# Moving a norm and an expert's sum to VectorE, and a setup loop into the first turn, of a hybrid S6 / mixture-of-experts / S5 kernel

## What is computed

```python
x = x + S6(layernorm(x))      # selective scan, then a norm with gamma and beta of its own
x = x + MOE(layernorm(x))     # 8 experts of hidden size 256, the two largest logits weigh them
x = x + S5(layernorm(x))      # diagonal complex scan with 64 states
x = x + MOE(layernorm(x))     # the same expert weights again
```

## Time and profile before

| | |
|---|---|
| median of 3 executions | 1848.97 us (1846.12 to 1856.43) |
| profiled execution | 1861.63 us, span of its instructions 1859.7 us |
| first scan to end of last | 55.05 to 1696.1 us |
| DVE / POOL busy | 1514.5 / 1513.9 us (81% each) |
| PE / ACT busy | 1351.0 / 1281.5 us |

### The profile page before, as it was taken

The page is one execution under the profiler, slowest core; times in us unless marked ns, Lnnn a source line. Parts: engine busy times, 40 slices in busy tenths (PEclk is TensorE's granted clock), DMA queues, the critical chain, the costliest instruction groups (busy, mean ns, idle before and its releaser), DMA issues.

```text
span 1859.7 us, 19053 instructions
## 1 busy us (share of the span) xinstructions
PE 1351.0 (73%) x5928; PEld 617.7 (33%) x5928; DVE 1514.5 (81%) x2105; ACT 1281.5 (69%) x2275; POOL 1513.9 (81%) x888
## 2 busy tenths in 40 slices
PE   4336458777886887778776878778787778668958
PEld 1001123234342343324342343324332343324535
DVE  4879988898889889898899888888888988895222
ACT  4547668687877778777777778777787777755423
POOL 0899999978998799977998899987998799983312
PEclk9557569889987989879897989879898898979979
DMA  3601411122111311132101401132111321100000
GB/s 87 212 34 71 164 46 51 49 91 97 57 40 48 148 51 33 54 104 96 55 25 50 162 29 51 49 106 81 51 51 49 102 85 52 46 29 1 7 1 6
DMA packets 38747, 121.89 MB, mean 66 GB/s; under 512 B 5875, under 2 KB 21110, under 8 KB 26358
## 3 DMA queue, kind: packets, MB, share of 16 engines
q1 hardware_dynamic: 37062, 120.67, 18.3%
q10 hardware_dynamic: 1584, 0.01, 0.0%
HBM read 109.13 MB, written 11.53 MB: 65 GB/s over the span
## 4 chain that ended last, share of the span: by engine, by line
PE 27%; ACT 18%; DVE 15%; POOL 14%; issue 8%; DVEq 0%; POOLq 0%; ACTq 0%
DVE h L1251 10%; POOL w L947 9%; PE bankH L565 8%; ACT da L837 5%; PE bankY L579 5%; PE bankG L565 5%; ACT yk L798 4%; ACT L837 3%; PE ys L633 2%; POOL x L890 2%; PE bankG L512 2%; DVE aq L1189 1%; PE bankY L559 1%; ACT L785 1%; ACT sq L785 1%
## 5 line engine op out<-in xcount | busy, mean ns | idle before, releaser
L1251 DVE TENSOR_TENSOR_SCAN h<-da,w 128x512 f32<-128x512 f32 x1024 | 1192.1, 1206 | 158.3 <-ACT da L837 133.0
L947 POOL TENSOR_TENSOR w<-ur,br 128x1024 f32<-128x1024 f32 x512 | 1193.6, 2365 | 33.1 <-DVE h L1251 21.2
L837 ACT ACTIVATE da<-dr,al 128x511 f32<-128x511 f32 x1024 | 681.9, 687 | 221.9 <-DVE h L1251 212.5
L633 PE MATMUL ys<-h,wsum 128*32 128x512 f32 x2048 | 320.9, 703 | 208.5 <-DVE h L1251 189.2
L565 PE MATMUL bankH<-nT,w 128*128 128x512 f32 x512 | 301.8, 673 | 89.7 <-DVE aq L1189 85.3
L890 POOL TENSOR_TENSOR x<-x,yk 128x512 f32<-128x512 f32 x128 | 163.1, 1274 | 211.2 <-ACT yk L798 210.6
L579 PEld LDWEIGHTS bankY<-w,aq 128*128 128x128 f32 x2048 | 262.8, 203 | 87.0 <-issue 65.0
L579 PE MATMUL bankY<-w,aq 128*128 128x128 f32 x2048 | 270.5, 289 | 12.4 <-DVE aq L1189 7.9
L565 PE MATMUL bankG<-nT,w 128*128 128x512 f32 x432 | 243.8, 648 | 24.6 <-DVE aq L1189 24.6
L798 ACT ACTIVATE yk<-bankY,rt 128x128 f32<-128x128 f32 x512 | 151.8, 364 | 121.5 <-PE bankY L579 107.8
L633 PEld LDWEIGHTS ys<-h,wsum 128*32 128x32 f32 x2048 | 42.9, 115 | 408.5 <-DVE h L1251 373.2
(11 more groups left out here) (187 smaller groups left out, 1135.8 us busy)
## 6 DMA issues: line engine op xcount, KB each, us to landing
br<-b_rows SPq DMA_DIRECT2D x64, 1024.0 KB, 5.0
dr<-d_rows SPq DMA_DIRECT2D x16, 1024.0 KB, 7.1
ur<-u_rows SPq DMA_DIRECT2D x16, 1024.0 KB, 8.4
d_rows<-vh SPq DMA_DIRECT2D x16, 256.0 KB
u_rows<-th SPq DMA_DIRECT2D x16, 256.0 KB
xnew<-in_L_attn_a_x_dram SPq DMA_DIRECT2D x8, 256.0 KB, 5.3
w<-in_L_ffn_W_dram SPq DMA_DIRECT2D x2, 1024.0 KB, 11.1
x<-in_L_attn_a_x_dram SPq DMA_DIRECT2D x8, 256.0 KB, 9.1
```

The costliest lines, as they stand in the source:

```text
L633: ins = nc.tensor.matmul(ys[32 * q:32 * q + 32, :], wsum[:, :], h[:, (DUOS * t.b + 2 * group + q // 2) % H_RING, q % 2, :], start=(n == 0) ...
L837: A(da[duo % D_RING][:, k % 2, 1:L], dr[:, half, q, 1:L], ACT.Exp, scale=nega[:, QUADS * half + q, n:n + 1]).then_inc(decay_ready, 1)
L947: G.tensor_tensor(w[:, turn_duo % W_RING, :, :], ur[:, half, q:q + 2, :], br[:, chunk % B_RING, row:row + 1, :].to_broadcast([128, 2, L]), ...
L1251: V.tensor_tensor_scan(h[:, turn_duo % H_RING, k % 2, :], da[duo % D_RING][:, k % 2, :], w[:, turn_duo % W_RING, k % 2, :], 0.0, ALU.mult, ...
```

## The change

It has five parts.

1. `normalize(1, ...)` leaves ACT: DVE does the four pieces itself at its slot 13, with `tensor_scalar` from SBUF to SBUF.
2. In the first MOE, expert 7 is no longer weighed by ACT and added by POOL: DVE does four `scalar_tensor_tensor` from bank Y onto `x1`, at slot 76.
3. The late tiles' second products (`g2_8`, `g2_9`) now stand ahead of output 3 in PE's order; outputs 3 and 4 go to slots 3 and 8, and their weighing and adding move with them.
4. The doubling loop moves out of the setup into slots 2 to 49 of turn 0, its helper rows into bank Y, and its one-element products become `tensor_scalar`. The rest of the S5 setup stands behind the two sums of line 1120. For the first sample POOL's `du` waits for two projections, not four.
5. `W3` is no longer halved. The routing gives true weights instead: one more small instruction on DVE (128 x 4), and the product with it now reads both inputs from SBUF.

```diff
-LATE_OUTPUTS = {3: 0, 4: 7, 5: 14, 6: 18, 7: 23}
+LATE_OUTPUTS = {3: 3, 4: 8, 5: 14, 6: 18, 7: 23}
...
-    at = silu_at(m, j) + step
-    return max(0, at - PAIRS) if is_late_tile(m, j) else at
+    at = silu_at(m, j)
+    return (max(0, at - PAIRS) if is_late_tile(m, j) else at) + step
...
-SETUP_AT = PRE_AT + 10
-MATRICES_AT = PRE_AT + 11
-TURN_AT = PRE_AT + 18
-SCALE_AT = 52
+SETUP_AT = PRE_AT + 17
+MATRICES_AT = PRE_AT + 17
+DOUBLE_AT = 2
...
-            def scale_outputs():
...
-                    G.tensor_scalar(part, part, 0.5, None, ALU.mult).then_inc(outputs_scaled, 1)
...
-                        for m in range(4):
+                        for m in range(2 if known(i, 1) else 4):
                             pool.wait_ge(drained[BANK[f"in{m}"]], t.before(f"in{m}") + 1)
...
+            def rotation():
...
                 while n < L:
-                    one, two = rT[:, 0:n], tq[:, 0, 0:n]
+                    yield DOUBLE_AT + 5 * n.bit_length()
+                    one, two = banks["Y"][:, 0:n], banks["Y"][:, 256:256 + n]
                     link(V.tensor_scalar(one, sinT[:, 0:n], s_, None, ALU.mult))
                     link(V.tensor_scalar(two, cosT[:, 0:n], s_, None, ALU.mult))
-                    link(V.tensor_tensor(S(19), s_, s_, ALU.mult))
-                    link(V.scalar_tensor_tensor(s_next, s_, 2.0, c_, ALU.mult, ALU.mult))
+                    link(V.tensor_scalar(S(19), s_, s_, None, ALU.mult))
+                    link(V.tensor_scalar(s_next, s_, c_, 2.0, ALU.mult, ALU.mult))
+                    yield DOUBLE_AT + 5 * n.bit_length() + 2
                     settle()
...
-                link(V.tensor_tensor(R(4), R(2), R(1), ALU.subtract))
-                link(V.tensor_tensor(R(5), R(2), R(1), ALU.add))
+                link(V.tensor_tensor(R(5), R(1), R(2), ALU.subtract))
                 yield SLOT[f"lg{m}"] + 5
                 v.wait_ge(gap_tanh_ready, 2 * c + m)
-                link(V.tensor_tensor(R(4), R(4), spread(rc[:, 2, :]), ALU.mult))
-                drain(f"lg{m}", V.tensor_tensor(rt[:, 0, :, :], R(4), R(5), ALU.add))
+                link(V.tensor_scalar(rc[:, 2, :], rc[:, 2, :], -0.5, 0.5, ALU.mult, ALU.add))
+                link(V.tensor_tensor(R(5), R(5), spread(rc[:, 2, :]), ALU.mult))
+                drain(f"lg{m}", V.tensor_tensor(rt[:, 0, :, :], R(5), R(2), ALU.add))
...
+                yield LN_AT[1] + NORM_LAG
+                v.wait_ge(rstd_ready[1], 4 * c + 4)
+                for a in range(TT):
+                    V.tensor_scalar(nrm[:, a, :], z[:, a, :], rs[:, 1, a:a + 1], nm[:, 1, a:a + 1], ALU.mult, ALU.add).then_inc(normed[1], 1)
...
+                last = f"y1_{E - 1}"
+                yield SLOT[last] + LAST_LAG
+                v.wait_ge(added, sums_before(c, 2))
+                p = got(t, last)
+                for a in range(TT):
+                    ins = V.scalar_tensor_tensor(x1[:, a, :], p[:, a * 128:(a + 1) * 128], rt[:, 0, a, E - 1:E], x1[:, a, :], ALU.mult, ALU.add)
```

More of the change, by code:

```diff
@@ L134, with sums_before, on_vector @@
 BANK = {name: bank for _, _, bank, name in PE_STEPS}
+def sums_before(c, m):
+    return SUMS * c + (E - 1) * (m - 1)
+def on_vector(m, e):
+    return m == 1 and e == E - 1
 def tiles_in(m, late):
@@ L167, in moe_act @@
                   + ([] if late else [(MOE_AT[m] + GAP_STEP, "gap", 0)])
-                  + [(weigh_slot(m, e, n), "y", 2 * e + n) for e in outputs_in(m, late) for n in range(2)],
+                  + [(weigh_slot(m, e, n), "y", 2 * e + n) for e in outputs_in(m, late) if not on_vector(m, e) for n in range(2)],
                   key=lambda s: s[0])
@@ L948, in pair @@
                                     br[:, chunk % B_RING, row:row + 1, :].to_broadcast([128, 2, L]), ALU.mult).then_inc(product_ready, 1)
[L950 removed]
+                weave(pair, [gates(t)] + tasks_of(t, pre_a, post, late))
             turns(pre_a, scan, post, late)
@@ L1205, in post @@
                 flat = lambda ap: ap[:, :, :].rearrange("p a c -> p (a c)")
+                last = f"y1_{E - 1}"
[4 more added lines that the diff above has]
+                    ins = V.scalar_tensor_tensor(x1[:, a, :], p[:, a * 128:(a + 1) * 128], rt[:, 0, a, E - 1:E], x1[:, a, :], ALU.mult, ALU.add)
+                    if a < TT - 1:
+                        ins.then_inc(last_added, 1)
+                drain(last, ins)
                 yield LN_AT[3]
-                v.wait_ge(added, E * (2 * c + 1))
+                v.wait_ge(last_added, (TT - 1) * (c + 1))
+                v.wait_ge(drained[BANK[last]], t.before(last) + 1)
                 yield from moments(3, c, LN_AT[3], x1)
```

41 lines of the change are left out of this document (19 added, 22 removed).

## The result

The changed kernel takes 1880.12 us (median of 4, 1873.73 to 1881.96) against 1852.70 for the kernel before in the same comparison. The ratio is 1.0137 with a 95% interval of 1.0104 to 1.0170, so it is slower by 19 to 31 us. The forecast was 5.5 us slower, with a range that ended at 1866: wrong in size. The profiled execution took 1881.96 us, its span is 1880.2. All medians here are over executions in the faster of the chip's two states; one execution of one experiment (1938.52 us, with both detours and the old order) fell into the slower one and is left out.

What follows compares the result with a forecast made beforehand. It took POOL to bound turn 0, neither DVE nor POOL to be full in turns 2 to 7, and chain length to count in the tail. -7.4 - 0.4 + 4.3 + 9.0 = +5.5 on 1848.97 gave 1854.5 us, range 1832 to 1866.

Steps and rivals of the forecast that it cites:

- The question that decided the sign: Whether small DVE instructions from SBUF to SBUF wait for POOL's running instruction; taken as yes, 128 x 4 waiting up to 2.34 us.
- The first two rivals: Small instructions not blocked: 1830.7 us, chance 0.18; only the routing's two-tensor product waits: 1841.2 us, chance 0.15.
- Slots 0 to 26: Turns 2 to 7, norm moved and late steps reordered: -1.7 us a turn, bounds +1.2 and -2.5.
- `z` +0.1: Turns 2 to 7: `z` waits for bank Y until output 3 is weighed, moving its sum by +0.1 us.
- The credit for the norm: Slot 14: ACT loses a 1.64 us norm, DVE's pieces fit its wait, scan 14 comes 1.6 us earlier.
- Turn 0: POOL loses 6.1 us of halvings, DVE gains the loop: 166.6 us, -0.4, bounds 163 and 173.
- DVE needs 151.2 + 12: Turn 0: DVE's busy time plus the doubling loop, 163.2 us before remaining waits.
- Routing: Turns 2 to 7: first routing +2.6 us (bounds +0.2, +4.7), second +1.2 (+0.2, +3.5); turn 1's routings 3.8.
- The third rival: At slot 13 the norm's pieces alternate with POOL's products: 2.8 us a turn more, 1871 us, chance 0.12.
- Slot 76: DVE's 1.88 us wait for POOL's last sum replaced by four pieces of 1.25: -0.6 us a turn, bounds -1.2 and +1.
- The start: Before the first scan: first sum and `du` run earlier, first scan at 47.7, -7.4 us, bounds -3 and -9.
- Turn 1: No long DVE wait at slot 13: norm shows with 1.1, routings 3.8, slot 76 gives 0.6, +4.3 us.

Runs made afterwards that it cites:

- both detours and the old order: Changed kernel, blend and `rT` routed through PSUM, norm on DVE, outputs 3 and 4 back at slots 0 and 7, output 3 before the late products: 1865.13 us, ratio 1.0059.
- the run with three products: Changed kernel plus three matmuls of a zero matrix with W1 in PE's pause at the end of turns 1 to 7: 1872.40 us, ratio 1.0101.
- the kernel with both detours: Changed kernel with the routing's 128x4 result written to PSUM and `rT` made in PSUM, then copied to SBUF: 1840.60 us, ratio 0.9928.
- the routing alone: Kernel before with only W3 unhalved and the 128x4 instruction and product from SBUF: 1889.90 us, ratio 1.0215.
- the norm on ACT without detours: Changed kernel with the attention norm back on ACT, routing blend and `rT` still in SBUF: 1876.99 us, ratio 1.0131.
- both detours with the norm on ACT: Changed kernel, routing blend and `rT` through PSUM, attention norm back on ACT: 1837.76 us, ratio 0.9931; with three zero products added, 1829.77 us, ratio 0.9883.
- the other detour: Changed kernel with the routing's 128x4 instruction writing its result into bank Y in PSUM: 1848.92 us, ratio 0.9982.
- the old order: Changed kernel with output 3 at slot 0 ahead of g2_8 and g2_9, and output 4 at slot 7: 1904.25 us, ratio 1.0291.
- the start alone: Kernel before with `du` waiting for two projections and the S5 setup behind the two sums, doubling loop still in the setup: 1848.33 us, ratio 0.9989.
- eight: Changed kernel plus eight matmuls of a zero matrix with W1 in PE's pause at the end of turns 1 to 7: 1894.94 us, ratio 1.0240.

## Why the prediction was wrong in size, point by point

The table in the first section gives the miss of the two profiled executions, +20.5 for +5.5, as 15.0 us. Split once more, at scan 32 of turns 2 to 7, it is: slots 0 to 32 of these six turns +10.2 (forecast -10.2, measured 0.0), the rest of these turns 0.1 (forecast +19.2, measured +19.3), turn 0 +4.5, turn 1 +4.1, start -2.7, tail -1.2. The medians are 22 us off, because the profiled execution of the kernel before lies 8.9 us above its median and that of the changed one 1.8. So two terms failed most: the gain of slots 0 to 26, and turn 0.

- **The question that decided the sign** was answered rightly: a small DVE instruction with its operands in SBUF alone waits for POOL's running instruction, in the one-tensor form too. The first two rivals (1830.7 and 1841.2) are out, by the rows of 2.00 and 2.29 us and by the 31 us that one PSUM operand gave back.
- **Slots 0 to 26**, -1.7 a turn, is the step that failed by most. In turn 3 scan 26 came 0.7 earlier, and by scan 32 nothing was left. The step "`z` +0.1" holds at the full clock (13.13 for 13.25), and so does the term: in the run with three products, in turn 3, scan 14 stands at 25.30 (1.63 before that of before) and scan 26 at 43.65 (2.4 before). Over six turns that run is 9.4 us ahead at scan 32, of the 10.2 forecast, and turns 2 to 7 are 10.5 shorter than in the changed kernel. What failed was the silent assumption that TensorE's clock would stand where it stood: in the changed kernel `z` came at least 1.4 us late in all six turns. What the low clock costs in a whole run is shown less well. The medians differ by 7.7 us with intervals that overlap; on the kernel with both detours they do not differ, and with the norm on ACT the 8.0 us between the medians are not the clock's by the traces. Why it fell in every turn of the changed kernel and in none of before is open: the routing alone shows it in five of these six turns, the norm on ACT without detours in all six, both detours in four, both detours with the norm on ACT in two at the turn's start, and the pause before it is 2.88 us in all.
- **The credit for the norm** was misplaced. At the full clock, with the norm on ACT, scan 14 is 1.5 us later than on DVE, scan 26 the same (43.81 and 43.65), and scan 32 is 0.5 earlier (53.51 and 54.00); at the low clock scan 32 is 2.1 earlier (55.1 and 57.2 in turn 3). So the norm's move earns nothing by scan 32, and beside the low clock it costs. What is earned in slots 0 to 26 comes with the new order: with the norm on ACT and the clock full in both, scan 26 is at 43.81 in the one and at 46.02 in the kernel before. That it is the order's alone is inferred, since no run has the new order by itself.
- **Turn 0**, "DVE needs 151.2 + 12": I carried the loop's 13.57 us over, gave back the two waits seen in it, and did not ask which of its instructions would meet POOL in turn 0. `rT` was the one left with both ends in SBUF, 5.71 us. With it mended turn 0 took 165.8 to 166.9, where 166.6 was forecast. In the whole run that is worth 8.3 us beside the other detour and 3.2 without it, where the intervals overlap; the traces show 4 to 5 of it, in turn 0.
- **Routing**, +2.6 and +1.2 a turn, 26.6 us in seven turns: measured 31 as a whole. In turn 3 the first cost 4.1 for 2.6, the second 1.5 for 1.2, and slot 76 gave most of the difference back. What failed in the first was carrying POOL's boundaries over from the trace of before. The change moved POOL by 0.7 us against the turn and so the first wait from 0.5 to 2.0 us. The range of the term (0.2 to 4.7) held it in the changed kernel, even for the wait through two products in turn 4 (4.32 us, and then the product's free 0.19); the 6.15 us seen with the norm on ACT went past it.
- **The third rival** (alternating pieces, 1871) did not come true in the changed kernel, for the reason given: POOL's late sum stood behind. Its condition and its rows were seen with the old order. There scan 14 is 2.7 us later than at the full clock with the new order, the 2.8 that the rival had; the whole runs differ by 24 us, of which the rival's 17 is a part at most.
- **Slot 76**, -0.6 a turn: right in sign, too small where it stands. Scans 73 to 87 gained 1.7 in turn 3. Of the part's 9.8 us between medians little lies in turns 2 to 7 (2.5 in the traces).
- **The start**, -7.4 (first scan 47.7): right in its mechanism. First scans stood at 44.5 to 48.4 in all kernels with both changes; the -10.1 of the changed kernel's execution is beyond the bound of -9 by the early logarithms. It needs the loop moved, as the start alone shows.
- **Turn 1**, +4.3, was 8.4 in the profiled execution: the first routing cost 3.5 there, scans 54 to 78 1.7 more (6.25 for 4.57), the second routing and ACT's last weighings behind it 2.2. But the runs with eight and with three products, the same in that turn, have +4.1 and +3.6, which is the forecast. So what was over there belongs to the execution, and why it varies is open.

The misses of the single terms are read in one pair of executions, the repairs were measured on several kernels; that both point to the same terms is the evidence, not that their sums fit.

By the Trainium skill's page "SBUF — State Buffer", section "Who interferes with whom", this exclusion was to be expected, of `rT` too: a `tensor_scalar` in a two-port mode and a DVE instruction with two SBUF inputs contend with GpSimd, and one with at most one SBUF input, outside these modes, does not. The trace agrees: the product took 2.29 us with both inputs in SBUF and 0.19 with one of them in PSUM, and the 128 x 4 before it 2.00 us and 0.16 with its output in PSUM.

## What to carry to other kernels

When a DVE instruction moves into a stretch where GpSimd is busy, go through it operand by operand: with all of them in SBUF even a 128 x 4 costs what GpSimd's instruction has left (the one-element `tensor_scalar` did not), and one operand in a free corner of PSUM takes that away. Price such a wait by the whole length of GpSimd's instruction (the phase that the old trace shows is gone once anything ahead has moved), and let the bound go up to where GpSimd next stands still. Before a microsecond is credited to a chain that begins behind a pause of PE, look at how long PE's first matmuls behind it take, and forecast a second case with them at half speed.
